# Routed gate and up product of an expert layer with the weights as the stationary operand, copied to a fixed buffer

## What is computed

```python
logits = x @ gate_w
top_id = jnp.argmax(logits, axis=-1)
score = jax.nn.sigmoid(jnp.max(logits, axis=-1, keepdims=True))
xs = x * score
g = jnp.einsum('th,ehi->eti', xs, rt_gate)      # 8 experts, 128 -> 256
u = jnp.einsum('th,ehi->eti', xs, rt_up)
y = jnp.einsum('eti,eih->eth', jax.nn.silu(g) * u, rt_down)   # 256 -> 128
routed = jnp.einsum('eth,te->th', y, jax.nn.one_hot(top_id, 8))
shared = (jax.nn.silu(x @ sh_gate) * (x @ sh_up)) @ sh_down
out = shared + routed
```

## Time and profile before

| | us |
|---|---|
| median of 3 runs | 884.05 |
| lowest, highest | 882.87, 887.5 |
| profiled execution, its time | 888.12 |
| profiled execution, its span | 886.3 |
| TensorE matmul busy in the span | 817.5 (92%) |
| VectorE, ScalarE, GpSimd busy | 651.5, 535.7, 250.6 |
| mean granted TensorE clock | 0.979 of full speed |

### The profile page before, as it was taken

How to read it: one execution, slowest core, us unless ns; L and a number is a source line. 1 busy time by engine, 2 the same in 40 slices (tenths; PEclk the granted TensorE clock), 3 DMA queues, 4 the chain that set the end, 5 groups by cost and what they waited for, 6 DMA issues and landing times.

```text
span 886.3 us, 14989 instructions
## 1 busy us (share of the span) xinstructions
PE 817.5 (92%) x4208; PEld 615.1 (69%) x4249; DVE 651.5 (74%) x1701; ACT 535.7 (60%) x931; POOL 250.6 (28%) x328
## 2 busy tenths in 40 slices
PE   4899998887689979999999999999999999999997
PEld 3677776675566656767777777777777777777775
DVE  4578778876564325577888888888888888889774
ACT  2365565644333323436677768776877777777765
POOL 1112111167817744211132223212321332131000
PEclk9899999999889989999999999999999999999999
DMA  5225674553234433210000000000000000000000
GB/s 144 58 82 149 177 208 129 166 139 112 69 95 130 142 98 104 84 49 24 13 25 25 1 24 24 24 0 24 24 24 0 24 24 21 3 24 13 13 1 24
DMA packets 91422, 55.66 MB, mean 63 GB/s; under 512 B 13440, under 2 KB 88184, under 8 KB 91256
## 3 DMA queue, kind: packets, MB, share of 16 engines
q1 hardware_dynamic: 74304, 40.38, 16.1%
q0 software_dynamic: 4096, 8.40, 3.3%
q10 hardware_dynamic: 12983, 6.41, 2.6%
HBM read 32.10 MB, written 23.07 MB: 62 GB/s over the span
## 4 chain that ended last, share of the span: by engine, by line
PE 32%; DVE 24%; issue 15%; POOL 14%; ACT 10%; DMA 2%; DVEq 1%; another core or an unknown queue 1%; POOLq 0%; ACTq 0%; SPq 0%
POOL x_sorted L502 6%; PE PS L746 5%; POOL rs L487 4%; DVE sil_l L1398 4%; DVE dec L1382 3%; PE PS L764 3%; DVE xn_c L1078 3%; DVE st L1067 3%; PE PS L997 3%; PE PS L999 3%; PE PS L998 3%; ACT sil L703 2%; PE PS L1019 2%; PE PS L1021 2%; PE PS L1020 2%
## 5 line engine op out<-in xcount | busy, mean ns | idle before, releaser
L703 ACT ACTIVATE sil<-PS,b_in_c 128x512 f32<-128x512 f32 x256 | 162.2, 685 | 113.3 <-PE PS L1006 72.0
L1398 DVE TENSOR_TENSOR sil_l<-sil,sil_h 128x512 fp32r<-128x512 f32 x256 | 164.7, 685 | 44.6 <-ACT sil_h L711 43.8
L485 POOL TENSOR_TENSOR ve<-mv,eps 128x4 f32<-128x4 f32 x64 | 17.5, 273 | 499.5 <-DVE mv L1072 499.5
L711 ACT ACTIVATE sil_h<-sil 128x512 fp32r<-128x512 f32 x224 | 128.9, 631 | 0.0
L1019 PE MATMUL PS<-sil_h,wout_l 128*128 128x512 f32 x256 | 117.9, 460 | 1.6 <-DVE sil_l L1398 1.6
L1382 DVE TENSOR_SCALAR dec<-PS,b_in_c 128x512 bf16<-128x512 f32 x128 | 95.5, 746 | 25.3 <-PE PS L999 23.5
L997 PE MATMUL PS<-x4T_h,win_l 128*128 128x512 f32 x256 | 102.4, 400 | 1.6 <-ACT yo L663 0.7
L1021 PE MATMUL PS<-sil_h,wout_h 128*128 128x512 f32 x256 | 100.6, 393 | 0.0
L1020 PE MATMUL PS<-sil_l,wout_h 128*128 128x512 f32 x256 | 100.2, 391 | 0.0
L999 PE MATMUL PS<-x4T_h,win_h 128*128 128x512 f32 x256 | 99.8, 390 | 0.0
L998 PE MATMUL PS<-x4T_l,win_h 128*128 128x512 f32 x256 | 99.8, 390 | 0.0
(11 more groups left out here) (153 smaller groups left out, 1593.9 us busy)
## 6 DMA issues: line engine op xcount, KB each, us to landing
x_sorted<-zeros SPq DMA_DIRECT2D x4, 1280.0 KB, 7.2
xs_in<-x_sorted SPq DMA_DIRECT2D x20, 256.0 KB
y_sorted<-yo ACTq DMA_DIRECT2D x20, 256.0 KB
X<-in_x SPq DMA_DIRECT2D x16, 256.0 KB
rows<-xn SPq DMA_DIRECT2D x16, 256.0 KB
xs<-rows SPq DMA_DIRECT2D x16, 256.0 KB
out<-res SPq DMA_DIRECT2D x16, 256.0 KB
ctxT<-in_ctx_t SPq DMA_DIRECT2D x16, 240.0 KB
```

What stands on the lines that cost most here:

```text
L703: act.activation(tile(sil[p % 2], c, W), bank(2 * (p % 2) + c), ACT.Silu, bias=b_in_c[:, 2 * p + c:2 * p + c + 1]).then_inc(t_silu, 1)
L711: act.activation(tile(sil_h[p % 2], c, W), tile(sil[p % 2], c, W), ACT.Copy).then_inc(t_hi, 1)
L1398: dve.tensor_tensor(tile(sil_l[p % 2], c, W), tile(sil[p % 2], c, W), tile(sil_h[p % 2], c, W).bitcast(F32), ALU.subtract).then_inc(t_lo, 1)
```

## The change

The weights of the two tiles of a pair are copied by VectorE from the array of all experts (`WGU`) into one of two fixed buffers (`w_now[v]`, 2 x 512 columns), and TensorE takes them from there as the stationary operand, 128 columns at a time, with the turned rows `xsT` (128 columns) moving. The result has features on partitions, which is what the down product needs, so `r_turn_act`, its PSUM bank and `r_evac_a` are gone, and `ract` is read by the down product itself. VectorE reads the packed experts for itself (`experts_of(dve, ...)`), and has one copy step for each pair (`r_weights`). `r_gate_up` waits for the copy (`r_w`), the copy waits until the pair before in that buffer is through (`r_gu_ps`), and `r_mul` waits for the down product that read its buffer (`r_y_ps`). On VectorE a round is now `r_first(r)`: experts of r + 1, copies for pair 2r + 2, product of pair 2r, and `r_second(r)`: copies for pair 2r + 3, product of pair 2r + 1. The early pieces of phase c stand between the two halves and behind the second, as before. The arena of SBUF grows by 4 KB for each partition.

```diff
@@ -211,9 +211,9 @@
         xsT = cut.two("xsT", W)
+        w_now = cut.two("w_now", 2 * 2 * FI)
         sg = cut.two("sg", 2 * FI)
         ract = cut.two("ract", 2 * FI)
-        actT = cut.two("actT", 2 * FI)
         yo = cut.two("yo", W)
@@ -750,19 +755,16 @@
-            def experts_of(r):
-                word = pe.value_load(cols(EXPERTS, r, 1)[0:1, :], min_val=0, max_val=E ** G - 1)
-                return [(word // E ** t) % E for t in range(G)]
-            def r_gate_up(q, v, r, u, experts):
+            def r_gate_up(q, v, r, u):
...
                 pe.wait_ge(r_xT, r + 1)
+                pe.wait_ge(r_w, q + 1)
                 if not below(q, 2):
...
                 for t in range(2):
-                    i = pe.matmul(bank(1 + 2 * v + t), tile(xsT[u], 2 * v + t),
-                                  cols(WGU, experts[2 * v + t] * (2 * FI), 2 * FI), start=True, stop=True)
+                    for n in range(2 * FC):
+                        i = pe.matmul(tile(bank(1 + 2 * v + t), n), tile(w_now[v], 2 * FC * t + n),
+                                      tile(xsT[u], 2 * v + t), start=True, stop=True)
                 i.then_inc(r_gu_ps, 1)
@@ -922,18 +924,12 @@
-            def r_turn_act(q, v):
+            def r_down(q, v, experts):
                 pe.wait_ge(r_act, q + 1)
-                if not first(q):
-                    pe.wait_ge(r_aT, q)
-                turn(bank(5), ract[v], P, P, r_aT_ps)
-            def r_down(q, v, experts):
-                pe.wait_ge(r_aT, q + 1)
                 for t in range(2):
                     for c in range(FC):
-                        i = pe.matmul(tile(bank(6), 2 * v + t), tile(actT[v], 2 * t + c),
+                        i = pe.matmul(tile(bank(6), 2 * v + t), tile(ract[v], FC * t + c),
                                       cols(WD, experts[2 * v + t] * (FC * P) + c * P, P), start=(c == 0), stop=(c == FC - 1))
@@ -942,15 +938,14 @@
                 if not end:
-                    coming = experts_of(r + 1)
+                    coming = experts_of(pe, r + 1)
                     r_turn(r + 1, 1 - u)
-                r_turn_act(q, 0)
                 if not first(r):
...
                 if not end:
-                    r_gate_up(q + 2, 0, r + 1, 1 - u, coming)
+                    r_gate_up(q + 2, 0, r + 1, 1 - u)
                 if now is None:
-                    now = experts_of(r)
+                    now = experts_of(pe, r)
                 if isinstance(r, int):
@@ -958,22 +953,21 @@
                         c_turn_x(1)
-                r_turn_act(q + 1, 1)
                 if not first(r):
...
                     return now
-                r_gate_up(q + 3, 1, r + 1, 1 - u, coming)
+                r_gate_up(q + 3, 1, r + 1, 1 - u)
                 return now, coming
...
-            r_gate_up(1, 1, 0, 0, first_experts)
+            r_gate_up(1, 1, 0, 0)
             r_body(0, 0, None, first_experts)
             with pe.Fori(0, HR // 2) as i:
-                now, coming = r_body(2 * i + 1, 1, experts_of(2 * i))
+                now, coming = r_body(2 * i + 1, 1, experts_of(pe, 2 * i))
                 r_body(2 * i + 2, 0, now, coming)
             pe.wait_ge(routed, 2)
-            now, coming = experts_of(HR), None
+            now, coming = experts_of(pe, HR), None
             for r in range(HR + 1, NR - 1):
@@ -1114,6 +1108,15 @@
+            def r_weights(q, v, experts):
+                if not below(q, 2):
+                    dve.wait_ge(r_gu_ps, q - 1)
+                for t in range(2):
+                    i = dve.tensor_copy(tile(w_now[v], t, 2 * FI),
+                                        cols(WGU, experts[2 * v + t] * (2 * FI), 2 * FI))
+                i.then_inc(r_w, 1)
@@ -1128,6 +1131,11 @@
                 if route == "all":
+                    dve.wait_ge(w_exp, 48)
+                    dve.wait_ge(routed, 1)
+                    experts = experts_of(dve, 0)
+                    r_weights(0, 0, experts)
+                    r_weights(1, 1, experts)
                     a_choose(1)
@@ -1314,15 +1322,9 @@
                 if not below(q, 2):
-                    dve.wait_ge(r_aT_ps, q - 1)
+                    dve.wait_ge(r_y_ps, q - 1)
                 pair = by_tile(PS[:, 512 * (1 + 2 * v):512 * (3 + 2 * v)], 512)
...
-            def r_evac_a(q, v):
-                dve.wait_ge(r_aT_ps, q + 1)
-                if not below(q, 2):
-                    dve.wait_ge(r_y_ps, q - 1)
-                dve.tensor_copy(actT[v], bank(5)).then_inc(r_aT, 1)
@@ -1332,22 +1334,29 @@
-            def r_half(q, v):
-                r_mul(q + 1, 1 - v)
-                r_evac_a(q, v)
+            def r_first(r):
+                coming = experts_of(dve, r + 1)
+                r_weights(2 * r + 2, 0, coming)
+                r_mul(2 * r, 0)
+                return coming
+            def r_second(r, coming):
+                r_weights(2 * r + 3, 1, coming)
+                r_mul(2 * r + 1, 1)
...
             a_first_slots(1)
-            r_mul(0, 0)
-            r_half(0, 0)
+            coming = r_first(0)
             a_slots(1)
-            r_half(1, 1)
+            r_second(0, coming)
             a_pack(1)
-            with dve.Fori(1, HR + 1) as r:
-                r_half(2 * r, 0)
-                r_half(2 * r + 1, 1)
-            for r in range(HR + 1, NR - 1):
-                r_half(2 * r, 0)
+            dve.wait_ge(routed, 2)
+            with dve.Fori(1, HR) as r:
+                coming = r_first(r)
+                r_second(r, coming)
+            for r in range(HR, NR - 1):
+                coming = r_first(r)
                 if r == FIRST_EARLY:
```

More of the change, by code:

```diff
@@ L137, in program @@
         WORK = TREE_W + EXPERT_W
-        ARENA = WORK + 10240
+        ARENA = WORK + 11264
         arena_base = -(-nc.sbuf_base // 32) * 32
@@ L259, in program @@
         r_in, r_out = sems("r_in", 2), sems("r_out", 2)
-        r_xT_ps, r_xT, r_gu_ps, r_sg, r_act, r_aT_ps, r_aT, r_y_ps, r_y = (sem(n) for n in (
-            "r_xT_ps", "r_xT", "r_gu_ps", "r_sg", "r_act", "r_aT_ps", "r_aT", "r_y_ps", "r_y"))
+        r_xT_ps, r_xT, r_w, r_gu_ps, r_sg, r_act, r_y_ps, r_y = (sem(n) for n in (
+            "r_xT_ps", "r_xT", "r_w", "r_gu_ps", "r_sg", "r_act", "r_y_ps", "r_y"))
         y_in, stored = sems("y_in", 2), sems("stored", 2)
@@ L286, in slots, with experts_of @@
             return tensors[h][bass.ds((r - h * HR) * W, W), :].rearrange("(t p) d -> p t d", p=P)
+        def experts_of(eng, r):
+            word = eng.value_load(cols(EXPERTS, r, 1)[0:1, :], min_val=0, max_val=E ** G - 1)
+            return [(word // E ** t) % E for t in range(G)]
         def first(g):
@@ L826, in a_body @@
                     pe.wait_ge(routed, 1)
-                    first_experts.extend(experts_of(0))
+                    first_experts.extend(experts_of(pe, 0))
                     pe.wait_ge(a_x1, NG)
                     pe.wait_ge(a_lg, NG)
-                    r_gate_up(0, 0, 0, 0, first_experts)
+                    r_gate_up(0, 0, 0, 0)
                     a_count(1)
@@ L1372, in _ @@
                     c_norm3(1)
-            r_half(2 * NR - 2, 0)
-            r_evac_a(2 * NR - 1, 1)
+            r_mul(2 * NR - 2, 0)
+            r_mul(2 * NR - 1, 1)
             def t_decide(g, p):
```

## The result

The changed kernel takes **880.3 us** (median of 7 runs, 878.99 to 880.76), the kernel before in the same job 886.04 (882.35 to 887.5). The ratio is 0.9944, 95% interval 0.9925 to 0.9964, so 3 to 7 us less. A second set of 6 runs gave 878.5 against 884.05: 0.9932 (0.9909 to 0.9954). The forecast was 883.5, range 877 to 890.5, with "no change" as the likeliest case. The time lies in the range, but the gain (0.56%, interval 0.36 to 0.75%) is just past the 0.5% that was called no change, and one term of the sum was four times too large.

The account below looks back on a forecast made before the run. The scatter on GpSimd was taken to bound the first half, TensorE the second, from 326.60 us to the trees. Scatter start +0.2, scatter pace +5.8 and second half -6.5 gave -0.5 us: 884.05 to 883.5 us, range 877 to 890.5.

Parts of the forecast that it names:

- The first half is not on the path: First ten routed rounds: done early by 5 us already, so savings there only lengthen TensorE's wait, to some 18 us.
- The round on TensorE: One routed round (body) on TensorE from 326.60 us on: 5.84 us against 6.54, 0.70 saved.
- From the resume to the trees: Second half of the routed rounds, 326.60 to 404.95 us, where TensorE sets the pace: -6.5 us.
- up to the passes for pair 28: Resume to gate and up of pair 28: 1.0 us late, copies queued behind `xn_c`, although bodies 9 to 12 gained 2.7.
- rest of body 13 and bodies 14 to 16: TensorE after the stall: 4.94 us for 5.32 (-0.4), then 19.7 for 22.75 (-3.0).
- bodies 17 to the trees: Bodies 17 to 19 and the last eviction, set by VectorE's chain: about 16.2 us for 20.28, -4.1.
- The stall: TensorE at gate and up of body 13, waiting for copies queued behind `xn_c`: 2 to 4 us, ended by `w_now`.
- The start of the scatter: Copies and loads on VectorE ahead of the second scatter, mostly covered by other waits: +0.2 us, 2.6 if nothing were covered.
- The pace of the scatter: VectorE's 38 copies hold GpSimd's indirect DMAs during the scatter: +5.8 us, units of 7.8 us instead of 7.1.
- rival B: Scatter: each copy holds GpSimd's DMA in full, +16.0 us, 893.8 us, slower; chance 0.08.
- rival A: Scatter: copies this short do not hold GpSimd, units stay at 7.1 us, 877.8 us; chance 0.17.
- The sum: Whole kernel: +0.2 + 5.8 - 6.5 = -0.5 us, carried to the median as 883.5 us.

Follow-up runs that it names:

- before again: The kernel before the change, run once more with no edit to get a second profile; 883.38 us, one run.

## Why the prediction was right in its range, and wrong in one term

- **The first half is not on the path.** Right: TensorE waited there for the load of the sorted rows before and after. That it would be free at 315 and wait some 18 us was wrong: it was free at 319.0 and waited 5.09, no longer than before (5.00). The first-half rounds run at 6.7 us on average (turns at 264.93 and 311.69, seven rounds), where they took 6.9 (266.10 to 314.38), not at 5.84. So the slack is 5 us, and the transposes put back there used up more than that. Why the rounds are that long is not settled, see the end.
- **The round on TensorE.** Right: 5.85 us against 5.84, sixteen passes in 1.84 and 1.78 from start to start (338.81 to 340.65, 341.55 to 343.33), predicted 1.80; the weight loads hide. Moved by itself (transposes back, second half) it is worth 4.9 to 6.2 us.
- **From the resume to the trees.** Predicted -6.5, measured -6.8 in the first profile (71.58) and -5.4 in the second (72.80). By its own parts: up to the passes for pair 28 predicted +1.0, measured -0.5 in the first (29.47 us behind the resume against 30.00) and +0.7 in the second (30.68; of the 1.2 us between the two, 1.1 lies in the first round); rest of body 13 and bodies 14 to 16 predicted 4.94 and 19.7, measured 4.98 and 19.78; bodies 17 to the trees predicted 16.2, measured 17.35 in both, so 1.1 us of gain too many. That the first profile comes so near to -6.5 is luck: two errors cancel in it. In the second they do not. The stall was there, 1.83 and 0.83 us (2.66, of the 2 to 4 named), behind the queue that was named, though its larger part already in body 12, and ended by the product behind the copies and not by `w_now`; the gather took 13.68 us to the roots for 13.44 before, +0.2 where the step had +1.2, the same overestimate as in the scatter.
- **The start of the scatter.** Predicted +0.2, measured +0.24, once before has a second profile. From the two first profiles alone one would have read -1.8.
- **The pace of the scatter.** This step failed: "+5.8 us", by position 0.125 a copy, by the casts 0.17. Measured +1.3 to +1.5 (57.69 and 57.78 against 56.40 and 56.28), about 0.04 a copy; two more of the 38 copies start only behind the last DMA. The prices came from two casts of 1.22 us back to back; a copy is a third of that. For the casts the price is not too high: in the gather of after the same two lie over one DMA, which took 2.30 us, 2.31 in the second profile, where the same DMA took 0.95 before. The copies cost less than their share of it: of the thirteen DMAs of the scatter beside which a copy ran, seven took the 0.97 us (1.03 for the first of a unit) that they take before, and six 0.06 to 0.18 more. Of the 1.3, 0.8 lies in the DMAs (31.4 to 32.2) and 0.5 in GpSimd's own small copies of slots and scores (240 and 211 ns each where they took 198 and 190); the longest, 0.48, is the one at 261.55, beside the pair of copies at 261.22. None of it grew into a full hold, so rival B is out, and rival A (nothing at all) is nearer than the forecast, but not it either. Why a short copy costs a smaller part of its time than a long cast is not shown.
- **The sum.** +0.2, +1.4 and -6.1 (mean of the two profiles) make -4.5, against -5.7 and -5.5 of the medians, whose intervals reach to -3.2. The forecast's -0.5 is off by the scatter term, 4.4 of the 5 us. The measured 880.3 lies about midway between the forecast, 883.5, and rival A, 877.8; the range held because it was wide enough for a scatter term between these two, not because the sum was right.
- **By the Trainium skill** (SBUF — State Buffer, Who interferes with whom) VectorE's two-port modes and GpSimd exclude each other. The direction agrees with the runs: copies on VectorE lengthen the scatter, 56.3 to 57.7 to 59.0, on ScalarE hardly, 56.6. The size here is about a tenth of the copies' own time. That it is this exclusion that lengthens the scatter is not shown by a run of its own.

What remains open: the part of the doubled copies' time that its profile lacks; and where the difference lies between the 3.6 to 4.9 us that LG to trees gained against before again and the 5.7 of the medians, if it is one.

## What to carry to other kernels

Where one stage waits for another engine, work taken off ahead of the wait buys nothing, and work taken off behind it buys nearly all of itself, less what falls into waits: find the last release and price only what follows. The reverse test, work added ahead of the wait, says little once it is longer than the wait. A price for contention taken from long instructions need not scale down to short ones; double the suspected instruction and remove it, and read the slope. And an engine that idles for some microseconds may pay again when it resumes: here 1.8 us of a slow first round and 0.6 behind it, bought back with transposes that nobody reads, sized to end just ahead of the data.

## What the runs showed of the hardware beyond this

- TensorE's granted clock fell after waits of 2.94 to 6.54 us in this stretch (0.50 to 0.79 in the 5 us window with most of the first passes) and stayed at 1.00 after a wait of 0.39 us, and where there was no wait. A fill that ended early did not keep the clock: waits of 2.94 and 6.32 us behind it still had slow first rounds, 7.48 and 7.91 us.
- In the first half of after, silu on ScalarE and the copies on VectorE, both waiting for the first gate and up of a round, start within 0.2 us of each other in four of the rounds, 1.7 to 2.9 us after the recorded end of those passes (passes 286.66 to 288.71, silu 291.64, copies 291.80), while in most rounds of the second half silu starts 0.04 us after them. TensorE's row shows no idle time in between. It was seen with the copies on either engine, but was under 0.6 us with doubled copies, and 0.04 in the rounds of before but one. No run was made for it, and its cause stays open; that it is part of what keeps first-half rounds at 6.7 us is likely, not shown. At 307.13 and 314.29 gate and up itself waits too, 1.07 and 1.11 us for the eviction of the turned rows on ScalarE.
- Two copies of 128x512 fp32 from SBUF to SBUF take 0.76 us where GpSimd is idle (329.15, 331.88, 335.17 in after), and 0.80 to 1.03 us in six of the seven pairs that start beside its scaling (1.03 at 270.28): the wait goes both ways.
